# The transform along H from sums and differences of row halves, on eight tiles of the array, with changes in the prologue and in front of conv2

## What is computed

```python
def diag_imp_conv_fft(x, B, h):          # B: 3x3 taps of one channel
    ...
    t = 1.0 / (h * (Bh.real ** 2 + Bh.imag ** 2) + 1.0)
    xh = jnp.fft.fft2(x)
    return jnp.real(jnp.fft.ifft2(xh * t[None])).astype(x.dtype)
...
for j in range(K.shape[0]):              # four layers
    Kj = project(K[j]); Lj = project(L[j])
    z = conv3x3(x, Kj)
    z = jax.nn.relu(batchnorm(z, gamma[j], beta[j]))
    x = x + h * conv3x3T(z, Kj)
    x = batchnorm(x, gamma[j], beta[j])
    x = diag_imp_conv_fft(x, Lj, h)
```

## Time and profile before

| | |
|---|---|
| median of three runs | 787.32 us (786.62 to 787.52) |
| the profiled execution, its own time | 783.87 us |
| its span (first to last instruction) | 782.0 us |
| mean granted clock of TensorE | 0.972 of full speed |
| TensorE busy | 741.6 us, 95% of the span |
| VectorE busy | 479.6 us, 61% |
| ScalarE busy | 387.5 us, 50% |
| POOL busy | 95.6 us, 12%, in the prologue alone |
| HBM traffic over the span | 21 GB/s |

### The profile page before, as it was taken

How to read it: one execution, slowest core, us unless ns; L and a number is a source line. 1 busy time by engine, 2 the same in 40 slices (tenths; PEclk the granted TensorE clock), 3 DMA queues, 4 the chain that set the end, 5 groups by cost and what they waited for, 6 DMA issues and landing times.

```text
span 782.0 us, 14876 instructions
## 1 busy us (share of the span) xinstructions
PE 741.6 (95%) x6016; PEld 374.5 (48%) x6016; DVE 479.6 (61%) x911; ACT 387.5 (50%) x703; POOL 95.6 (12%) x92
## 2 busy tenths in 40 slices
PE   4779999999999999999999999999999999999995
PEld 1223333222454875224558753235677542355785
DVE  2587887764957852448668533397676333877661
ACT  1465666636622655257135543491446433823564
POOL 0376666830000000000000000000000000000000
PEclk9798999999999999989999999999999998999998
DMA  9991111248000132840000427500004274000034
...
DMA packets 44645, 51.16 MB, mean 65 GB/s; under 512 B 36385, under 2 KB 36514, under 8 KB 42530
## 3 DMA queue, kind: packets, MB, share of 16 engines
...
## 4 chain that ended last, share of the span: by engine, by line
PE 81%; DVE 10%; ACT 3%; issue 2%; DMA 1%; SPq 1%; POOL 0%; DVEq 0%; ACTq 0%; POOLq 0%
PE psum L887 39%; PE psum L1068 7%; PE psum L1039 7%; PE psum L961 6%; PE psum L1057 6%; PE psum L1023 6%; PE psum L910 3%; PE psum L1012 2%; PE psum L949 2%; DVE work L824 2%; DVE tabT L808 2%; DVE spare L824 2%; ACT Z L543 1%; PE psum L926 1%; DVE X L815 1%
## 5 line engine op out<-in xcount | busy, mean ns | idle before, releaser
L887 PE MATMUL psum<-Z,wts 128*32 128x512 f32 x1536 | 177.4, 615 | 5.1 <-DVE Z L801 5.1
L887 PE MATMUL psum<-X,wts 128*32 128x512 f32 x1536 | 170.1, 593 | 0.2 <-DMA X<-X 0.2
L824 DVE COPY work<-psum 64x256 f32<-64x256 f32 x224 | 94.5, 422 | 22.9 <-PE psum L1023 15.9
L734 DVE BATCH_NORM_STATS2 stats<-Z 128x6 f32<-128x512 f32 x60 | 41.5, 692 | 106.8 <-ACT Z L483 106.7
L887 PEld LDWEIGHTS psum<-Z,wts 128*32 128x32 f32 x1536 | 49.5, 112 | 118.3 <-issue 107.6
L887 PEld LDWEIGHTS psum<-X,wts 128*32 128x32 f32 x1536 | 47.4, 109 | 105.5 <-issue 103.1
L483 ACT ACTIVATE Z<-psum 128x512 f32<-128x512 f32 x64 | 38.3, 598 | 118.1 <-PE psum L887 107.0
L543 ACT ACTIVATE Z<-Z,small 64x128 f32<-64x128 f32 (+3 forms) x92 | 85.0, 973 | 5.2 <-DVE small L792 4.7
L568 ACT ACTIVATE work<-psum 64x256 f32<-64x256 f32 x160 | 61.4, 384 | 34.7 <-PE psum L1057 22.5
L815 DVE SCALAR_TENSOR_TENSOR X<-psum,X 128x512 f32<-128x512 f32 x64 | 43.7, 683 | 47.4 <-PE psum L887 47.0
L1057 PEld LDWEIGHTS psum<-cstS,work 128*128 128x128 f32 x512 | 58.4, 192 | 9.8 <-issue 9.8
...
## 6 DMA issues: line engine op xcount, KB each, us to landing
...
```

The source lines that it names most:

```text
L824: last = nc.vector.tensor_copy(dst, src)
L887: last = nc.tensor.matmul(out_b[C * r:C * r + C, :], weights[:, o:o + C], rows(src, reg, bp, g, CH, dj - 1), start=(dj == 0), stop=(dj == ...
```

## The change

- `fwdH` is made of sums and differences. VectorE forms, behind `turn`, the sum and the difference of the two halves of the rows (`fold_turned`, for quarters 2 and 3; ScalarE copies quarters 0 and 1). The even frequencies depend on the sums alone, the odd ones on the differences alone, so each product has 32 rows and 64 columns of weights. A pair's forward transform is 16 products with 496 columns in two rounds of eight tiles; the second round adds to the first in the same four banks, and slot 0 (now two products of 32 columns) stands between the rounds. The constants are sorted to fit.
- All four banks are claimed before the first round. VectorE's product with the table takes two instructions per bank, each on 64 partitions, and four for slot 0.
- `by_dve`: ScalarE takes the odd quarters of fwdW for the first two pairs, and invH's odd quarters for the second and third pair. In `turn`, ScalarE's copies fall from four to two a pair, and VectorE has four additions.
- The step `slot0c` of the third pair comes behind invW of the first. Scale and bias of the second norm come before VectorE's slot 0 of the third pair. In the last layer half of invW of the third pair comes before invH of the fourth.
- In front of conv2: each table product becomes two column tiles of 64 over all 128 rows (the rows beyond 12 hold zeros in the constants, and the taps are prepared on 128 partitions). VectorE makes all of the first pair's relu in the form Z2, in three pieces; ScalarE makes Z0 in three pieces, and conv2's first chunks wait for a piece each. The table's reciprocal comes in four parts behind conv2 chunks 1, 3, 5 and 6.
- In the prologue: 16 matmuls of 96x96 on the weights w1, whose result nobody reads, as soon as w1 is in; a one-column Prelu on ScalarE before the first result; ScalarE's copy of the second hidden result behind the first three cuts; and the third hidden product behind the spreads of chunk 1.

```diff
-    steps += fourier(j, 3, "turn") + [("norm", j, 2)] + fourier(j, 2, "fwdH")
-    steps += fourier(j, 0, "invW") + fourier(j, 3, "fwdW") + fourier(j, 2, "invH") + fourier(j, 1, "invW")
+    steps += fourier(j, 3, "turn") + [("norm", j, 2)] + fourier(j, 2, "fwdH")[:-1]
+    steps += fourier(j, 0, "invW") + [("slot0c", j, 2)]
+    steps += fourier(j, 3, "fwdW") + fourier(j, 2, "invH") + fourier(j, 1, "invW")
     steps += fourier(j, 3, "fwdH")
     rest = {1: fourier(j, 3, "invH"), 3: fourier(j, 2, "invW"), 5: fourier(j, 3, "invW")}
+    if j == DEPTH - 1:
+        rest = {1: quarters("invW", j, 2, (0, 1)) + fourier(j, 3, "invH") + quarters("invW", j, 2, (2, 3)),
+                5: fourier(j, 3, "invW")}
...
-    return q % 2 == 0 if stage == "fwdW" and bp >= 2 else stage == "fwdW" or bp >= 1 and q % 2 == 1
+    return q % 2 == 0 if stage == "fwdW" else bp == 3 and q % 2 == 1
...
+        def folds(q):
+            return turned[:, :].rearrange("p (c f i) -> p c f i", f=2, i=SL)[:, :, :, 16 * q:16 * q + 16]
...
-            act.wait_ge(hconv_consts, 32)
+            act.wait_ge(hconv_consts, 16)
+            nc.scalar.activation(small[:, 24:25], b1S[:, 0:1], ACT.Prelu, alpha=LEAK)
             keep_hidden(0)
-            keep_hidden(1)
             exps(0)
             for i in range(3):
                 cut(0, i)
+            keep_hidden(1)
             keep_probs(0)
...
             def norm_relu(bp, g, n):
                 parts = [(Z0, REG, g, n, 0, 128)]
                 if g == 0:
                     parts.append((Z2, REG2, 0, 1, 2 * C, 128))
-                    if bp:
-                        parts.append((Z2, REG2, 1, n, 0, 128))
-                elif g + n < G:
-                    parts += [(Z2, REG2, g + 1, n, 0, 128)]
-                else:
-                    parts += [(Z2, REG2, g + 1, n - 1, 0, 128), (Z2, REG2, G, 1, 0, 2 * C)]
+                if bp:
+                    parts.append((Z2, REG2, g + 1, min(n, G - 1 - g), 0, 128))
+                if g + n == G:
+                    parts.append((Z2, REG2, G, 1, 0, 2 * C))
                 for t, reg, g, n, p0, p1 in parts:
                     z = rows(t, reg, bp, g, n, 0, p0, p1)
                     last = nc.scalar.activation(z, z, ACT.Relu, bias=small[p0:p1, 13:14], scale=small[p0:p1, 12:13])
...
+                if bp == 0:
+                    norm_relu(bp, CH, CH)
+                    norm_relu(bp, 2 * CH, G - 2 * CH)
+                else:
+                    norm_relu(bp, CH, G - CH)
...
-                dst = turned[:, :].rearrange("p (c h) -> p c h", h=H)[:, :, 16 * q:16 * q + 16]
-                nc.scalar.activation(dst, bank(n).rearrange("p (h c) -> p c h", c=C),
+                nc.scalar.activation(folds(q)[:, :, 0], bank(n).rearrange("p (i c) -> p c i", c=C),
...
+                for g, n in ((1, CH), (1 + CH, CH), (1 + 2 * CH, G - 1 - 2 * CH)):
+                    z = rows(Z2, REG2, 0, g, n)
+                    link(nc.vector.tensor_scalar(z, z, S(12), S(13), ALU.mult, ALU.add))
+                    nc.vector.tensor_scalar(z, z, 0.0, None, ALU.max).then_inc(relu_by_dve, 1)
+            def add_squares(j):
                 for i in range(4):
                     bk.result(NUMBER["table", j, i])
-                link(nc.vector.tensor_tensor(tabT[:, :], turned[:, 0:1024], turned[:, 1024:2048], op=ALU.add))
+                nc.vector.tensor_tensor(tabT[:, :], turned[:, 0:1024], turned[:, 1024:2048], op=ALU.add)\
+                    .then_inc(squares_read, 1)
+                dve.wait_ge(squares_read, j + 1)
                 link(nc.vector.tensor_scalar(tabT[:, :], tabT[:, :], STEP, 1.0, ALU.mult, ALU.add))
-                nc.vector.reciprocal(tabT[:, :], tabT[:, :]).then_inc(table_done, 1)
-                dve.wait_ge(table_done, j + 1)
+            def invert(i):
+                t = tabT[:, 256 * i:256 * i + 256]
+                nc.vector.reciprocal(t, t).then_inc(table_done, 1)
...
+            def fold_turned(j, c):
+                n, q = NUMBER["turn", j, c], c % Q - 2
+                bk.result(NUMBER["turn", j, c - 2])
+                bk.full(n)
+                t, b = folds(q), bank(n).rearrange("p (i c) -> p c i", c=C)
+                nc.vector.tensor_tensor(t[:, :, 1], t[:, :, 0], b, op=ALU.subtract)
+                nc.vector.tensor_tensor(t[:, :, 0], t[:, :, 0], b, op=ALU.add).then_inc(drained[n % BANKS], 1)
...
             def scale_fwdH(j, c):
-                n, q = NUMBER["fwdH", j, c], c % Q
+                n, (i, odd) = NUMBER["fwdH", j, c], divmod(c % Q, 2)
                 bk.full(n)
                 src = bank(n)[:, 0:16 * (SL - 1)].rearrange("p (c b s) -> p c b s", c=8, b=2)
-                tt = tabT[:, 8 * SL * q:8 * SL * (q + 1)].rearrange("p (c s) -> p c s", s=SL)[:, :, 1:SL]\
-                    .unsqueeze(2).broadcast_to([128, 8, 2, SL - 1])
-                to = spec[:, N * q:N * q + N].rearrange("p (c b s) -> p c b s", c=8, b=2)[:, :, :, 1:SL]
-                nc.vector.tensor_tensor(to, src, tt, op=ALU.mult).then_inc(drained[n % BANKS], 1)
+                for f in range(2):
+                    x, p = f ^ odd, slice(H * f, H * f + H)
+                    tt = table_of(x, f).rearrange("p (c s) -> p c s", s=SL)[p, 8 * i:8 * i + 8, 1:SL]\
+                        .unsqueeze(2).broadcast_to([H, 8, 2, SL - 1])
+                    o = N * (i + 2 * x)
+                    to = spec[:, o:o + N].rearrange("p (c b s) -> p c b s", c=8, b=2)[p, :, :, 1:SL]
+                    last = nc.vector.tensor_tensor(to, src[p], tt, op=ALU.mult)
+                last.then_inc(drained[n % BANKS], 1)
...
+            pe.wait_ge(w1_in, 16)
+            for i in range(WARM):
+                nc.tensor.matmul(bank(NUMBER["logits", 1])[0:3 * C, 0:3 * C], w1S[:, :], w1S[:, :], start=True, stop=True)
             pe.wait_ge(zeroed, 1)
-            pe.wait_ge(hconv_consts, 32)
+            pe.wait_ge(hconv_consts, 16)
...
-                e = (C_ERE, C_EIM)[i // 2]
-                nc.tensor.matmul(bank(n), cm(e, k=12), taps[:, N * (i % 2):N * (i % 2) + N], start=True,
-                                 stop=True).then_inc(filled[n % BANKS], 1)
+                odd = i % 2
+                e = (C_ERE, C_EIM)[i // 2] + H * odd
+                for k in range(2):
+                    last = nc.tensor.matmul(bank(n)[H * k:H * k + H, :], cm(e, H), taps[:, N * (k ^ odd):N * (k ^ odd) + N],
+                                            start=True, stop=True, tile_position=(0, H * k))
+                last.then_inc(filled[n % BANKS], 1)
...
-                if c == 0:
-                    pe.wait_ge(relu_by_dve, j + 1)
-                if c % Q < 2:
-                    pe.wait_ge(relu_done, 2 * BP * j + 2 * (c // Q) + 1 + c % Q)
+                bp, q = divmod(c, Q)
+                if bp == 0 and q < 3:
+                    pe.wait_ge(relu_by_dve, 3 * j + q + 1)
+                    pe.wait_ge(relu_done, (2 * BP + 1) * j + q + 1)
+                elif q < 2:
+                    pe.wait_ge(relu_done, (2 * BP + 1) * j + 2 * bp + q + 2)
...
             def forward_h(j, c):
-                n, q = NUMBER["fwdH", j, c], c % Q
-                bk.claim(n)
-                bk.result(NUMBER["fwdW", j, c])
-                nc.tensor.matmul(bank(n)[:, 0:16 * (SL - 1)], cm(C_FH),
-                                 freqw[:, N * q:N * q + N].rearrange("p (a s) -> p a s", s=SL)[:, :, 1:SL],
-                                 start=True, stop=True).then_inc(filled[n % BANKS], 1)
+                if c % Q:
+                    return
+                bp = c // Q
+                for i in range(Q):
+                    bk.claim(NUMBER["fwdH", j, c + i])
+                    bk.result(NUMBER["fwdW", j, c + i])
+                for second in range(2):
+                    for part in range(2):
+                        i = second ^ part
+                        for f in range(2):
+                            n, p = NUMBER["fwdH", j, c + 2 * i + f], H * part + SL * f
+                            for x in range(2):
+                                o, to = N * (i + 2 * x), H * (x ^ f)
+                                last = nc.tensor.matmul(bank(n)[to:to + H, 0:16 * (SL - 1)], cstS[p:p + SL, C_FH:C_FH + H],
+                                                        freqw[p:p + SL, o:o + N].rearrange("p (a s) -> p a s", s=SL)[:, :, 1:SL],
+                                                        start=(second == 0), stop=(second == 1), tile_position=(p, to))
+                            last.then_inc(filled[n % BANKS] if second else first_parts, 1)
+                    if not second:
+                        slot_0(j, bp)
+                        pe.wait_ge(first_parts, 4 * (BP * j + bp + 1))
```

131 lines of the change are left out of this document (87 added, 44 removed).

## The result

The changed kernel takes 806.28 us (median of 4 runs, 802.1 to 808.07) against 786.97 (785.08 to 787.52) of the kernel before on the same chip: 1.0242 times as long, interval 1.0199 to 1.0285. It is slower, by some 2%, and outside the predicted range. The profiled execution took 808.07 us with a span of 806.3 and a mean granted clock of 0.955 (before 0.972). It is the slowest of the four, and the profiled 783.87 of the kernel before lies 3 us under the median, so sizes read between these two traces add up to 24.3 us where the medians differ by 19.3.

What follows compares the result with a forecast made beforehand. The prediction took TensorE, busy 741.6 of 782.0 us, to bound the kernel. Its terms, -8.0 + 12.9 - 7.7 + 1.2 - 5.0 = -6.6 us, bring the median from 787.32 to 780.7, range 767 to 790.

Steps and rivals of the forecast that it cites:

- transform, first and second pair: Transform along H: 2.5 us instead of 3.82, net 1.0 saved a pair, -8.0 us over four layers.
- third and fourth pair, three layers: Layer's end: waits for ScalarE's copies make this stretch 2.9 us longer in each of three layers, +8.7.
- the same, last layer: Last layer, without a conv1 behind: the transform starts 4.3 us late, the end takes 15.2, +4.2.
- clock behind the waits: Behind the 2.6 us wait before the third transform the clock may fall: 0.3 a layer, +1.2 us, at most 6.8.
- clock in front of conv2: Table products over 128 rows instead of 12 keep the clock at 2.4 GHz when conv2 starts: -7.7 us.
- prologue: Before the layers: moved ScalarE work and dummy matmuls bring the turned probabilities forward to 22.4 to 24.5 us: -5.0.
- VectorE's halves: VectorE's products with the table: 0.60 us each on 64 partitions, as on 128, so eight take 4.8.
- both waits: TensorE waits for ScalarE copies before the third transform (2.6 us) and before the fourth (1.9).
- (a): Third and fourth pair: VectorE and ScalarE keep up better, the stretch costs nothing, 767.8 us; chance 0.17.
- (c): Second pair's stage: ScalarE's copies run a tenth longer and the second transform waits too, 790.7 us; chance 0.12.
- (b): In front of conv2: the clock falls all the same, 7.7 us are missing, 788.4 us; chance 0.13.
- (d): New transform: two tiles of one row group don't run together, +1.8 us a transform, 795 us; chance 0.06.

Runs made afterwards that it cites:

- fill_both: The changed kernel with 11 and 7 products that nobody reads put into the waits before the third and fourth transforms: 792.19 us, 1.0075 of the kernel before.
- joined_12_rows: The kernel before with only the prologue and front-of-conv2 changes, its table products on 12 rows again: 779.93 us, 0.9921 of the kernel before.

## Why the prediction was wrong, point by point

Measured on spans, the change was to give -6.6 us and cost +24.3, a miss of 31 (by the medians +19.3, a miss of 26). By its own steps (their measured sum is 24.7; the rest lies behind the last product):

| term | forecast | measured | from |
|---|---|---|---|
| transform, first and second pair | -8.0 | -0.5 | A: 66.27 - 66.39, four layers |
| third and fourth pair, three layers | +8.7 | +14.3 | conv1: 36.33 - 31.57 |
| the same, last layer | +4.2 | +7.3 | fourth +5.4, L +1.9 |
| clock behind the waits | +1.2 | +15.7 | after against fill_both |
| clock in front of conv2 | -7.7 | -8.9 | 588.0 against 782.0 - 185.13 = 596.9 |
| prologue | -5.0 | -3.2 | conv2 of the first layer, 181.93 against 185.13 |

**The step that failed** is the term for the clock behind the new wait, the last paragraph on the clock: "It would slow work that waits for VectorE anyway (products can't start before 16.3), so I price it at 0.3 a layer". It fell in every layer as that sentence allowed, but in three it fell a second time, behind the wait of 1.9 us, which the sum had forecast without a question about its clock. There nothing waits for VectorE: the transform grows from 3.18 to 4.22 us, conv1's first two convs from 5.36 to 7.58. And the first fall was not covered either: the fourth transform starts at 34.78 instead of 33.15. In the second layer that is 1.63 before it, 1.04 in it, and 2.23 in E (60.96 against 58.73), 4.9 in all. Even the stated upper bound of 6.8 was under half of the 15.7: it took one fall a layer at 1.7 us, which is what half clock for 3.4 us costs, and measured were seven falls, six of them 6.8 us long.

The Trainium skill (TensorE: Matmul & The Clock Gate, the section on HAM oscillation) says that gaps between bursts let the gate close. The traces here agree, at up to two places of each layer, 15.7 us in all; the section's own case has waits of about 3 to 5 us, and here 2.8 and 1.9 were enough. The prediction named that rule for the first wait alone and let its own price stand.

**Mis-sized: the transform.** It takes 3.15 us, not 2.5. The rounds take 1.02 and 1.12 (0.88 assumed), slot 0 between them 0.57 (0.35), behind them 0.44 (0.25). The four pieces together stand 0.8 us above my 0.88, 0.35, 0.88 and 0.25, where I had put 0.1 for changing the tiles. A good third of it is slot 0's weights. Slot 0 is now two products instead of one, each in two passes, and every pass loads all 128 columns; the weight loads of slot 0 in the kernel before, and of a round and of slot 0 in the changed one, read:

```profile
378.05 0.30 PEld L1032 LDWEIGHTS psum<-work,cstS 128*128 128x128 f32 x2 [0.84 <-issue]
```

```profile
379.41 0.23 PEld L1131 LDWEIGHTS psum<-work,cstS 32*64 32x64 f32 x16 [0.84 <-issue]
...
380.43 0.52 PEld L1108 LDWEIGHTS psum<-work,cstS 128*128 128x128 f32 x4 [0.78 <-issue]
```

Four loads that start 0.11 apart make the 0.44 behind the rounds by themselves, and most of the 0.57. What is left, 0.14 and 0.24 in the rounds and 0.13 behind slot 0, lies where the tiling changes: each round lies between such changes, while the six rounds of the two convs from which I took 0.88 have them only at their ends. The Trainium skill (TensorEngine Tiling, Key Properties) says that a change of the mode drains TensorE. Those 0.5 us agree with it, but no run here shows the drain by itself. Behind the turn conv2 waits 0.52 to 0.58, not 0.3. So 0.65 + 0.25 of the 1.0 a pair went, 7.2 us over eight pairs.

**Mis-sized: VectorE's halves.** I took 0.60 for a product on 64 partitions. Eight in a row take 5.53 us, 0.69 each, where four on all 128 took 2.41:

```profile
429.45 0.79 DVE L884 TENSOR_TENSOR work<-psum,tabT 64x32 f32<-64x32 f32 x4
430.30 5.53 DVE L899 TENSOR_TENSOR work<-psum,tabT 64x496 f32<-64x496 f32 x8
```

The folds and the norm came as forecast (15.7 behind invH's start, forecast 15.8), the products at 16.5 to 22.0 instead of 16.3 to 21.1. With them the fourth transform comes 1.1 later than forecast (33.15), and its own length adds 0.7: 1.8 in three layers makes 5.4 of the 5.6 between forecast and measurement. In the last layer invH of the fourth pair waits twice for these products, 2.3 us, for which my 15.2 for the tail had next to nothing:

```profile
785.26 1.13 PE L1156 MATMUL psum<-cstS,work 128*128 128x128 f32 x8 [0.70 <-DVE work L899]
788.04 4.54 PE L1156 MATMUL psum<-cstS,work 128*128 128x128 f32 x24 [1.64 <-DVE work L899]
```

**Right:** both waits, their sizes and releasers; the clock in front of conv2, and that the 12 rows were the reason (joined_12_rows takes 778.5 - 181.96 = 596.5 from the first conv2 on, and so gives 8.5 of the 8.9 back); ScalarE's place in the prologue, with the turned probabilities at 23.34 (forecast 22.4 to 24.5). **Mis-sized there:** "What follows is held by VectorE and POOL in the same order, and moves along" did not hold. The turned probabilities came 4.4 us earlier and conv2 3.2, which is why 5.0 became 3.2.

**The rivals.** (a), smaller waits, and (c), ScalarE late in the second pair, didn't happen. (b) didn't, in front of conv2. (d) fell: the sixteen records of a round, eight tiles and two passes, end within 1.09 us, though two tiles share each row group. The rule of the Trainium skill behind it (TensorE: Matmul & The Clock Gate, Part 3, loads overlap only where the row group differs) is not borne out by the rows of loads above: all sixteen loads of a round lie within 0.23 us of its start, though its first pass, in the same rows of the array, runs for 0.6. None of the rivals was slow enough; the missing one was "the clock falls behind both new waits".
